# Four attention and feed-forward layers on one core: the last attention's probabilities turned by DMA in 16 bits, and feed-forward weights loaded inside the attentions

## The reference

```
x = x + attention0(norm(x), ctx)   # 32 heads of 128, 8 groups, rotated
x = x + gated_ffn(norm(x))
x = x + attention1(norm(x), ctx)   # 16 heads of 96, keys also from x
x = x + routed_lora_ffn(norm(x))
x = x + attention2(norm(x), ctx)   # 32 heads of 128, keys also from x
x = x + topk_rank_one_ffn(norm(x))
x = x + attention3(norm(x), ctx, mask)  # 32 heads of 16, 8 groups
x = x + int8_linear(int8_linear(norm(x)))   # 512 -> 2048 -> 512
attention3: softmax(where(mask, q k^T / 4, lowest)) v, then w_out
```

## Time and profile before

| | us |
|---|---|
| median of three runs | 1912.69 |
| the profiled execution | 1909.78 |
| its span, first to last instruction | 1908.0 |
| TensorE busy | 1752.3 (92%) |
| VectorE busy | 1422.7 (75%) |
| ScalarE busy | 1049.8 (55%) |
| Pool busy | 882.7 (46%) |

### The profile page before, as it was taken

The page is one execution under the profiler, slowest core; times in us unless marked ns, Lnnn a source line. Parts: engine busy times, 40 slices in busy tenths (PEclk is TensorE's granted clock), DMA queues, the critical chain, the costliest instruction groups (busy, mean ns, idle before and its releaser), DMA issues.

```text
span 1908.0 us, 28955 instructions
## 1 busy us (share of the span) xinstructions
PE 1752.3 (92%) x9892; PEld 1419.0 (74%) x9892; DVE 1422.7 (75%) x3036; ACT 1049.8 (55%) x1999; POOL 882.7 (46%) x863
## 2 busy tenths in 40 slices
PE   6899999999797999978899999999988999998988
PEld 5677777777576888757688888888866778776755
DVE  6777887878577887747677777778755587787898
ACT  5766667666125565631556556656641287775333
POOL 6776776664633232044343444343336632242762
PEclk9999999999899999998999999999998999998998
DMA  5656656565417999651589778889762200120210
GB/s 183 142 103 139 134 116 141 121 120 118 121 25 141 213 194 175 136 121 50 108 159 196 160 166 175 164 162 194 149 141 78 75 1 23 46 90 22 73 44 23
DMA packets 524177, 226.13 MB, mean 119 GB/s; under 512 B 493696, under 2 KB 503168, under 8 KB 516736
## 3 DMA queue, kind: packets, MB, share of 16 engines
q1 hardware_dynamic: 524032, 224.28, 53.9%
HBM read 97.08 MB, written 5.24 MB: 54 GB/s over the span
## 4 chain that ended last, share of the span: by engine, by line
PE 69%; DVE 17%; DMA 3%; ACT 3%; issue 3%; POOL 3%; SPq 1%; POOLq 0%; DVEq 0%; ACTq 0%
PE ps_t L339 9%; PE ps_t L340 8%; PE ps_t L341 8%; PE ps_s L339 8%; PE ps_s L340 7%; PE ps_s L341 7%; PE ps_o L339 4%; PE ps_o L340 3%; PE ps_o L341 3%; PE ps_o L1880 3%; PE ps_t L1911 3%; ACT ps_s L1247 2%; PE ps_s L1866 2%; DVE nmax L1277 2%; DVE ps_s L1274 1%
## 5 line engine op out<-in xcount | busy, mean ns | idle before, releaser
L1247 ACT ACTIVATE ps_s<-ps_s,nmax 128x768 f32<-128x768 f32 (+1 forms) x320 | 252.6, 789 | 342.0 <-DVE nmax L1277 239.5
L1220 ACT ACTIVATE l_ab<-ps_s,rinv 128x768 f16<-128x768 f32 (+1 forms) x320 | 260.8, 815 | 69.0 <-DVE rinv L1322 54.1
L1315 DVE SCALAR_TENSOR_TENSOR l_ab<-ps_s,rinv,l_ab 128x768 f16<-128x768 f32 (+1 forms) x320 | 289.1, 903 | 2.8 <-ACT l_ab L1220 2.4
L1277 DVE TENSOR_REDUCE nmax<-ps_s 128x1 f32<-128x768 f32 x192 | 183.5, 956 | 123.3 <-PE ps_s L341 122.9
L339 PE MATMUL ps_o<-l_pt,l_v 128*128 128x256 f16 (+1 forms) x832 | 230.9, 278 | 19.3 <-DMA l_v<-l_vab 9.2
L340 PE MATMUL ps_o<-l_pt,l_v 128*128 128x256 f16 (+1 forms) x832 | 229.6, 276 | 0.0
L341 PE MATMUL ps_o<-l_pt,l_v 128*128 128x256 f16 (+1 forms) x832 | 229.5, 276 | 0.0
L339 PE MATMUL ps_s<-l_k_hi,l_q_hi 128*128 128x512 f32 (+3 forms) x512 | 186.4, 364 | 21.9 <-DVE l_ab L1315 18.9
L377 POOL TENSOR_TENSOR wo_hi<-raw_big,one 128x512 fp32r<-128x512 f32 (+2 forms) x100 | 103.8, 1038 | 204.6 <-PE ps_t L341 123.6
L340 PE MATMUL ps_s<-l_k_lo,l_q_hi 128*128 128x512 f32 (+3 forms) x512 | 179.8, 351 | 0.0
L341 PE MATMUL ps_s<-l_k_hi,l_q_lo 128*128 128x512 f32 (+3 forms) x512 | 179.1, 350 | 0.0
(11 more groups left out here) (386 smaller groups left out, 4947.0 us busy)
## 6 DMA issues: line engine op xcount, KB each, us to landing
...
```

The costliest lines, as they stand in the source:

```text
L1220: e.activation(sp.ab[:, (k - 1) % 3, 0, :], self.scores_out(k - 1), ACT.Copy, scale=rinv[:, i:i + 1]).then_inc(s_pa, 1)
L1247: e.activation(self.scores_out(k), self.scores_out(k), ACT.Exp, bias=nmax[:, i:i + 1], scale=-1.0 if l.rope else 1.0, accum_out=rsum[:, i: ...
L1277: e.tensor_reduce(nmax[:, i:i + 1], o, AX.X, ALU.max, negate=True).then_inc(s_max, 1)
L1315: e.scalar_tensor_tensor(out=b, in0=self.scores_out(t), scalar=rinv[:, i:i + 1], in1=a, op0=ALU.mult, op1=ALU.subtract).then_inc(s_pb, 1)
```

## The change

Last attention: the transposes on TensorE go. Mask and exponential stay in the score bank, of which there are now five (`l3_bank`). ScalarE writes a 16-bit copy, scaled by 2^15, into one of six buffers `l3ab`, behind a wait on its own exponential; VectorE writes the rest in 16 bits; SyncE issues one DMA transpose a tile into one of six `l3pt`. The values too become two 16-bit parts, scaled by their largest magnitude, which a ones-by-diagonal product finds over the partitions; the output scaling takes the factor back. The values' and inverse sums' turns share one bank (`aside_bank`). Attention products run three slots later, projections two slots later. SyncE now goes through the tiles, so the loads of the last feed-forward layer are issued at tiles 72, 88 and 102, and two weight loads at 10 and 40.

The other layers: the first loads of each feed-forward layer are issued within the attention before it (steps N-7, N-2 or N-1), and `split_beside_norm` puts the powers of the norm on Pool after the second and the fourth split piece.

```
-        l3pt = [[at(f"l3_pt{i}_{n}", [P, 4, SQ], F32R, R0 + 8 + 8 * i + 4 * j) for j, n in enumerate(("hi", "lo"))]
-                for i in range(2)]
-        l3p = at("l3_p", [P, 6, SK], F32, R0 + 24)
+        l3pt = [at(f"l3_pt{i}", [P, 2, 8, P], F16, R0 + 8 + 4 * i) for i in range(6)]
+        l3ab = [at(f"l3_ab{i}", [P, 2, SK], F16, R0 + kb) for i, kb in enumerate((66, 68, 70, 72, 32, 34))]
...
-        l3v = [at(f"l3_v{i}", [P, 4, 640], F32R, R0 + 54 + 10 * i) for i in range(2)]
+        l3v = [at(f"l3_v{i}", [P, 4, 640], F16, R0 + 54 + 5 * i) for i in range(2)]
...
+                    if k in self.next_loads:
+                        self.next_loads[k](e)
...
         def f0_sp(e):
-            load(e, "q", c0.q, A["f0_w12"][0], ("o", c0.o))
...
+        def split_beside_norm(e, norm, n, used):
+
+            for half in range(2):
+                for piece in (2 * half, 2 * half + 1):
+                    split(e, "q", n, used, piece)
+                norm.pool_half(e, half)
+            e.wait_ge(s_xn, TT * (norm.i + 1))
+
         def f0_pool_first(e):
-            split_all(e, "q", c0.q, c0.g - 8)
+            split_beside_norm(e, norms[1], c0.q, c0.g - 8)
...
         def f1_sp(e):
-            load(e, "kv", c1.kv, A["f1_wa"], ("kv", c1.kv), cols=256)
-            load(e, "q", c1.q, A["f1_wb"], ("o", c1.o))
...
         def f2_sp(e):
-            load(e, "kv", c2.kv, A["f2_wr"], ("kv", c2.kv), cols=64)
-            load(e, "q", c2.q, A["f2_wa"][0], ("o", c2.o))
...
-                job(kind, blk, i, 4 * quad, 4 * quad, 4 * quad + 1, 4 * quad + 1)
+                job(kind, blk, i, 4 * quad + 2, 4 * quad + 2, 4 * quad + 3, 4 * quad + 3)
...
+        def l3_bank(i):
+
+            return (ring[0], ring[1], ring[2], ring[3], ps_t[0][:, :])[i % 5]
...
+            for k in range(1, N3 + 1):
+                i = k - 1
+                u = l3_unit(i)
+                e.wait_ge(s3["second_part"], i + 1)
+                if u >= 6:
+                    e.wait_ge(s3["pv"], u - 5)
+                e.dma_start_transpose(l3pt[u % 6][:, l3_tile(i)[3], :, :], l3ab[i % 6][:, :, :].rearrange("p a n -> p (a n)"))\
+                    .then_inc(s3_crossed[i % 6], 16)
+                if k == 10:
+                    load(e, "q", c3.q + 1, A["l3_wq"][1], ("o", c3.o + 1))
+                if k == 40:
+                    load(e, "o", c3.o + 1, A["l3_wo"][1], ("q", c3.q + 2))
+                if k in F3_LOADS_AT:
+                    f3_sp_ahead(e, F3_LOADS_AT.index(k))
...
+                pair = 2 * quad + qt
+                if pair >= 2:
+                    e.wait_ge(s3["second_part"], 2 * pair - 3)
...
-                e.wait_ge(s3["tlo"], lo_count3[piece_at3["t", u // 2 * 4 + 2 + u % 2]])
+                    e.wait_ge(s3["aside_free"], aside3["v", blk] + 1)
+                for i in (u // 2 * 4 + u % 2, u // 2 * 4 + u % 2 + 2):
+                    e.wait_ge(s3_crossed[i % 6], 16 * (i // 6 + 1))
                 if g == 0 and u:
                     e.wait_ge(s3["scaled"], u // 4)
                 for k in range(4):
                     for y in range(2):
-                        mm = e.matmul(ps_o[:, 0:SQ], l3v[blk % 2][:, k, g * P:(g + 1) * P], l3pt[u % 2][y][:, k, :],
+                        mm = e.matmul(ps_o[:, 0:SQ].rearrange("p (t q) -> p t q", t=2), l3v[blk % 2][:, k, g * P:(g + 1) * P],
+                                      l3pt[u % 6][:, :, 4 * y + k, :],
...
+                if k in (-5, 6):
+                    b = int(k == 6)
+                    o = take_aside(aside3["max", b])
+                    e.wait_ge(s3["vdiag"], b + 1)
+                    e.matmul(o[:, 0:P], l3ones[:, :], l3diag[:, :], start=True, stop=True).then_inc(s3["aside"], 1)
...
-                if k % 4 >= 2 and 0 <= k - 6 < N3:
-                    attend((k - 6) // 4 * 2 + k % 2)
+                    mm.then_inc(s3["aside"], 1)
+                if k % 4 in (1, 2) and 0 <= k - 9 < N3:
+                    attend((k - 9) // 4 * 2 + (k - 1) % 4)
...
-                if 0 <= k - 2 < N3:
-                    i = k - 2
-                    o = take_turn_bank(piece_at3["t", i])
-                    e.wait_ge(s3["exp"], i + 1)
-                    for kk in range(4):
-                        mm = e.transpose(o[:, kk * P:(kk + 1) * P], l3p[:, i % 6, kk * P:(kk + 1) * P], ident[:, :])
-                    mm.then_inc(s3["T"], 1)
...
-                if 0 <= k - 3 < N3:
-                    i = k - 3
-                    p, u, qt = piece_at3["t", i], l3_unit(i), l3_tile(i)[3]
-                    e.wait_ge(s3["T"], p + 1)
-                    if u >= 2:
-                        e.wait_ge(s3["pv"], u - 1)
-                    e.activation(l3pt[u % 2][0][:, :, qt * P:(qt + 1) * P],
-                                 ps_t[p % 2][:, :].rearrange("p (k q) -> p k q", q=P), ACT.Copy).then_inc(s3["thi"], 1)
...
-                    e.activation(l3p[:, k % 6, :], l3p[:, k % 6, :], ACT.Exp, bias=nmax[:, c:c + 1], scale=-1.0,
-                                 accum_out=rsum[:, c:c + 1]).then_inc(s3["exp"], 1)
+                    o = l3_bank(k)
+                    e.activation(o, o, ACT.Exp, bias=nmax[:, c:c + 1], scale=-1.0, accum_out=rsum[:, c:c + 1]).then_inc(s3["exp"], 1)
+                    if k >= 6:
+                        e.wait_ge(s3_crossed[k % 6], 16 * (k // 6))
+                    e.wait_ge(s3["exp"], k + 1)
+                    e.activation(l3ab[k % 6][:, 0, :], o, ACT.Copy, scale=P_SCALE).then_inc(s3["first_part"], 1)
...
+                    link(e.tensor_reduce(l3vmax[:, at], j.bank(), AX.X, ALU.max, apply_absolute_value=True))
                     e.tensor_copy(l3vs[:, j.blk, :], j.bank()).then_inc(s3["job_out"], 1)
...
-                e.tensor_tensor_reduce(out=l3p[:, i % 6, :], in0=ring[i % 4], in1=l3mask[:, qt, :],
+                o = l3_bank(i)
+                e.tensor_tensor_reduce(out=o, in0=o, in1=l3mask[:, qt, :],
...
+                if 0 <= k - 1 < N3:
+                    i = k - 1
+                    a, b = (l3ab[i % 6][:, part, :] for part in (0, 1))
+                    e.wait_ge(s3["first_part"], i + 1)
+                    e.scalar_tensor_tensor(out=b, in0=l3_bank(i), scalar=P_SCALE, in1=a, op0=ALU.mult, op1=ALU.subtract)\
+                        .then_inc(s3["second_part"], 1)
+                if k in (-4, 7):
+                    at = slice(int(k == 7), int(k == 7) + 1)
+                    e.wait_ge(s3["aside"], aside3["max", at.start] + 1)
+                    e.tensor_reduce(l3vlim[:, at], aside_bank[:, 0:P], AX.X, ALU.max).then_inc(s3["aside_free"], 1)
+                    e.wait_ge(s3["aside_free"], aside3["max", at.start] + 1)
+                    link(e.tensor_scalar(l3vlim[:, at], l3vlim[:, at], V_LEAST, None, ALU.max))
+                    e.tensor_scalar(l3vout[:, at], l3vlim[:, at], 1.0 / (P_SCALE * V_SCALE), None, ALU.mult)
+                    link(e.tensor_scalar(l3vdiv[:, at], l3vlim[:, at], 1.0 / V_SCALE, None, ALU.mult))
+                    e.reciprocal(l3vrec[:, at], l3vdiv[:, at]).then_inc(s3["vscale"], 1)
...
-                if 0 <= k - 3 < N3:
...
-                    e.tensor_tensor(pt[1], ps_t[p % 2][:, :].rearrange("p (k q) -> p k q", q=P), pt[0].bitcast(F32),
-                                    ALU.subtract).then_inc(s3["tlo"], 1)
...
-                    e.tensor_tensor(l3o[:, u % 2, :], ps_o[:, 0:SQ], l3r[:, u % 2, :], ALU.mult).then_inc(s3["scaled"], 1)
+                    e.scalar_tensor_tensor(out=l3o[:, u % 2, :], in0=ps_o[:, 0:SQ], scalar=l3vout[:, b:b + 1], in1=l3r[:, u % 2, :],
+                                           op0=ALU.mult, op1=ALU.mult).then_inc(s3["scaled"], 1)
...
+        F3_LOADS_AT = (72, 88, 102)
...
+        def f3_sp_ahead(e, step):
+
+            if step == 0:
+                e.wait_ge(s3["job_full"], find3["k", 3, 0].n + 1)
+                e.dma_start(q_b1[:, :], A["f3_b1"]).then_inc(s_lay, 16)
+                for stored in s_wout:
+                    e.wait_ge(stored, 8 * row_rounding.pieces)
+                for i in range(2):
+                    e.dma_start(q_w1[i][:, :, :], w1_ints[:, 2 * i:2 * i + 2, :]).then_inc(s_wback[0], 16)
+            elif step == 1:
+                e.wait_ge(w_rdy["o"], 8 * cf.o)
+                f3_load_chunk(e, 0)
+                e.dma_start(q_w2[:, :, :], w2_ints).then_inc(s_wback[1], 16)
+            else:
+                e.wait_ge(w_rdy["q"], 8 * (cf.q + 1))
+                f3_load_chunk(e, 1)
...
+        a0.next_loads[a0.N - 2] = lambda e: load(e, "q", c0.q, A["f0_w12"][0], ("o", c0.o))
+        a1.next_loads[a1.N - 7] = lambda e: load(e, "kv", c1.kv, A["f1_wa"], ("kv", c1.kv), cols=256)
+        a1.next_loads[a1.N - 1] = lambda e: load(e, "q", c1.q, A["f1_wb"], ("o", c1.o))
+        a2.next_loads[a2.N - 7] = lambda e: load(e, "kv", c2.kv, A["f2_wr"], ("kv", c2.kv), cols=64)
+        a2.next_loads[a2.N - 1] = lambda e: load(e, "q", c2.q, A["f2_wa"][0], ("o", c2.o))
...
             f0_pool_first(e)
```

(1 more changed line is left out.)

152 lines of the change are left out of this document (69 added, 83 removed).

## The result

| | before | after |
|---|---|---|
| median (20 runs each), us | 1912.68 (1909.63 to 1917.73) | 1908.07 (1903.54 to 1915.18) |
| profiled execution: time, span, us | 1909.78, 1908.0 | 1903.54, 1901.7 |
| TensorE's granted clock over the span | 0.972 | 0.953 |

The ratio is 0.9976, 95% interval 0.9966 to 0.9986: faster, by 4.6 us or 0.24%, clear of the noise but within the 5.7 us that the prediction counted as no change. 29.4 us were forecast, and 1908.07 lies outside the range of 1864 to 1902.

What follows compares the result with a forecast made beforehand. TensorE was taken to bound the last attention, Pool and its load the hand-overs. Gains of 8.4 and 21 us, 29.4 together, took the profiled 1909.78 to 1880.4; plus 2.9 for the median gave 1883, range 1864 to 1902.

Steps and rivals of the forecast that it cites:

- The step of the last attention: Last attention, time per tile: 1.49 us for the VectorE-ScalarE path plus 0.20 of other work, taken as 1.70, from 1.79.
- The gain of 11.4: Last attention's loop: 127 steps falling from 1.79 to 1.70 us save 11.4 us, bounds +34 and -20.
- rival A: Last attention gains nothing: extras add on both engines, steps of 1.82 us; 14 us gained in all, 1898; chance 0.20.
- The handshake: Last attention: copy, subtract, mask, exponential alternating between ScalarE and VectorE become the new bound, 2.98 us per two tiles, 1.49 each.
- Rival E: Last attention: TensorE, with 5.2 us of work in 6.8, is granted 1.2 GHz; 2.6 us a tile, 1995 us; chance 0.03.
- DMA, charged at 3 us: Last attention's loop: DMA transposes queued behind weight loads make ScalarE's copy wait, costing 3 us (0 to 8).
- Rival C: Last attention: DMA transposes pace the loop at 2.12 us a tile; 42 us lost, 21 gained, 1934; chance 0.06.
- Rival B: Last attention: extras hide and the DMA floor of 1.61 us a tile sets the pace; 44 us gained, 1869; chance 0.12.
- Start, 0.7: Before the last attention's first scores: value maximum, diagonal and small VectorE instructions, some 2 us, cost 0.7 us (0 to 2).
- Tail: End of the last attention: last mask to scaled output falls from 8.9 to 7.3 us; gain 0.7 (-2 to +2).
- Hand-overs, 21: Three attention-to-feed-forward hand-overs: earlier loads and Pool powers save 7, 7 and 8 us, less 1 behind: 21 (9 to 26).
- Rival D: Hand-overs: early loads delay the last DMA transposes by 3 to 5 us, so they bring only 10 us; 1894; chance 0.10.

Runs made afterwards that it cites:

- early_filler5: The changed kernel with the value-maximum product after the query projections, the 2 MB load after the loop, and five zero products before score waits; 1888.96 us.
- fixes: The changed kernel with Pool's splits held off the first-half scale, second hand-over's load after the last crossing, value-maximum product later, 2 MB load after the loop; 1907.67 us.
- handovers_only: The kernel before with only the three hand-overs changed, the last attention as before; 1895.31 us, ratio 0.9916.
- apart_handovers: The kernel before with only the hand-overs changed, Pool's splits kept off both scales, the second hand-over's load two crossings before the end; 1898.72 us.

## Why the prediction was wrong

**The step of the last attention (1.49 + 0.20, taken as 1.70).** What failed is the sentence that TensorE "stops being the bound as soon as another engine needs more". TensorE, waiting in the pairs of scores, was granted 0.80 over the loop, and at 1.2 GHz its remaining work is the longest again: busy 15.23 of 16.20 us in tiles 40 to 47. With zero products put into those waits the grant is 0.92 to 0.97 and the step 1.71 to 1.76, so the clock is the cause. The step was 1.84 with the crossings cut to an eighth. The gain of 11.4 became a loss of 7.6. The prediction's own sign of being wrong, masks 1.8 or more apart, came true; rival A's 1.82 is near the measured 1.85, but by another cause.

That 1.70 and the 1.71 to 1.75 of the kernels with fillers from the second pair on agree is in part luck. The handshake gives 1.57 in plain groups at full clock, less than forecast; the mean reaches 1.72 because some groups, those with new values or loads above all, take 1.8 to 2.1 a tile (early_filler5).

**Rival E had the mechanism, at 0.03.** I waved it off with the earlier trace rows, "0.99 over 190 us with the idle spread as thinly". That row speaks against using it so: there TensorE is busy 184.75 of 190 us. In the new loop at full clock it is busy 8.75 of 12.60. The row that should have warned me, and which I cited, is the stretch in the earlier trace rows that was granted 0.87 although TensorE was busy 12.02 of 13.00 us. Priced for the whole loop E gave 1995; a stretch that comes and goes (0.80 on the mean) belonged into the sum as a term. A mean of 0.80 is two fifths of the time at half clock; with the prediction's 2.6 us a tile there and 1.70 at full clock that is an estimated 1.97, with the measured 1.57 at full clock 1.87, and the loop had 1.85. The Trainium skill, TensorE: Matmul & The Clock Gate (A second HAM failure mode: psum-queue depth-cycling), describes this nearer than the section that the prediction quoted: short idle times between groups of matmuls, as the banks cycle, make the clock go up and down. By that rule the trace agrees: waits of 1.1 to 1.4 us for a bank, then half clock.

**DMA, charged at 3 us.** Right in kind for the 2 MB load at tile 88, but only with the clock held: 3.9 us. In the changed kernel it cost nothing, as fixes shows. Rival C is out. Rival B did not come about, but its floor is near: a DMA share of 0.96 runs beside 1.72.

**Start, 0.7.** It was 1.9, inside the bound. I had the instructions on VectorE right and missed TensorE's order: its wait of 1.80 us for the diagonal holds up the projections behind.

**Tail.** -0.7 forecast, +1.6 measured, inside the bound. Last mask to scaled output is 10.24 us (1734.51 to 1744.75) where 7.3 was taken. TensorE does not idle for the 3 us assumed, but works through output projections before and between its last sets of attention products, and the last set starts at 1743.67, 6.9 us behind VectorE's last subtraction at 1736.79.

**Hand-overs, 21.** 17.4 by the traces, 19.2 inside the hand-overs, 17.5 by handovers_only: the mechanism held (at the end the second power waits for VectorE and not for Pool, 0.97 us). By the inside measure the three gave 5.8, 6.8 and 6.7 for 7, 7 and 8. The term that was off is "VectorE's first-half scale is over at 492.9": that scale starts at 492.96, takes 2.67 us and not 1.00 beside Pool's split, and the additions wait behind it; 1.7 us each at the first and third. Rival D's mechanism is there at the second, where TensorE's wait for its crossing is 3.6 us longer (5.97 less 2.41), but it cost far less than that: 0.9 us to the last output products, and a later or earlier load, with the wait down to about 2.4, brought 2.0 (fixes) and 0.1 us (apart_handovers). The 1.4 that the sum took off there (8.4 to 7) was about right.
